# AdaLN block with gated linear attention: the six modulation vectors summed over their input rows on TensorE instead of on VectorE

## The reference

```python
mod = (silu(c) @ wmod).reshape(1, 6, 1, -1)          # wmod is 512 x 3072
sa, ca, ga, sb, cb, gb = (mod[:, n] for n in range(6))
ga = (2 * (ga >= 0) - 1) * maximum(abs(ga), 0.25)    # the same for gb
h = layernorm(x) * (1 + ca) + sa
x = x + ga * attention(h, Wq, Wk, Wv, Wo, Wg, Wog, Wd, bd, norm_w)
h = layernorm(x) * (1 + cb) + sb
x = x + gb * channel_mix(h, W_r, W_k, W_v, mu_r, mu_k)
```

## Time and profile before

| | us |
|---|---|
| median of three executions | 3675.05 |
| lowest and highest of them | 3674.24, 3677.36 |
| the profiled execution, its own time | 3674.58 |
| its span, first to last instruction | 3672.8 |
| PE busy | 3596.5 (98%) |
| DVE busy | 2145.5 (58%) |
| ACT busy | 1546.0 (42%) |
| POOL busy | 464.7 (13%) |
| mean granted clock of TensorE | 0.991 |

### The profile page before, as it was taken

How to read it: one execution, slowest core, us unless ns; L and a number is a source line. 1 busy time by engine, 2 the same in 40 slices (tenths; PEclk the granted TensorE clock), 3 DMA queues, 4 the chain that set the end, 5 groups by cost and what they waited for, 6 DMA issues and landing times. The chain is left out here.

```text
span 3672.8 us, 73725 instructions
## 1 busy us (share of the span) xinstructions
PE 3596.5 (98%) x25349; PEld 3339.3 (91%) x25349; DVE 2145.5 (58%) x5207; ACT 1546.0 (42%) x3904; POOL 464.7 (13%) x883
## 2 busy tenths in 40 slices
PE   7999999999999999999999997899999999999998
PEld 7999999999999999999999997688888888888887
DVE  4555555555555555555555556566566655666566
ACT  4445445445545445445445453333332323233332
POOL 0111111111111111111111111100000000000000
PEclk8999999999999999999999999899999999999999
DMA  4222322322322322322232223412221122212220
GB/s 156 76 60 65 81 60 58 87 62 56 87 63 55 86 64 54 81 71 54 75 77 54 75 71 87 162 69 71 77 91 69 69 80 85 75 69 74 75 91 23
DMA packets 206044, 274.89 MB, mean 75 GB/s; under 512 B 13968, under 2 KB 146080, under 8 KB 206000
## 3 DMA queue, kind: packets, MB, share of 16 engines
q1 hardware_dynamic: 206000, 274.31, 25.6%
HBM read 189.84 MB, written 84.41 MB: 75 GB/s over the span
## 5 line engine op out<-in xcount | busy, mean ns | idle before, releaser
L813 POOL TENSOR_TENSOR k_lo<-kg,k_hi 128x256 fp32r<-128x256 f32 x256 | 186.7, 729 | 1501.1 <-ACT q_hi L588 1501.1
L609 ACT ACTIVATE decay<-cum_rows,w_cur 128x128 f32<-128x128 f32 x1024 | 327.8, 391 | 20.6 <-POOL cum_rows L807 12.7
L55 PE MATMUL psJ<-h_hi,w_g_hi 128*128 128x256 f32 x1024 | 314.7, 307 | 8.3 <-DVE h_lo L675 4.6
L577 ACT COPY q<-psJ 128x256 f32<-128x256 f32 x256 | 95.5, 373 | 501.1 <-PE psJ L57 501.1
L55 PE MATMUL psJ<-h_hi,w_q_hi 128*128 128x256 f32 x1024 | 304.4, 297 | 0.0
L683 DVE SCALAR_TENSOR_TENSOR kg<-gate,psJ 128x256 f32<-128x256 f32 x256 | 107.8, 421 | 333.0 <-PE psJ L57 305.5
L56 PE MATMUL psJ<-h_lo,w_q_hi 128*128 128x256 f32 x1024 | 286.2, 279 | 0.0
L57 PE MATMUL psJ<-h_hi,w_k_lo 128*128 128x256 f32 x1024 | 286.1, 279 | 0.0
L56 PE MATMUL psJ<-h_lo,w_g_hi 128*128 128x256 f32 x1024 | 285.9, 279 | 0.0
L57 PE MATMUL psJ<-h_hi,w_q_lo 128*128 128x256 f32 x1024 | 285.8, 279 | 0.0
L55 PE MATMUL psJ<-h_hi,w_k_hi 128*128 128x256 f32 x1024 | 285.6, 279 | 0.0
(11 more groups left out here) (226 smaller groups left out, 10601.8 us busy)
## 6 DMA issues: line engine op xcount, KB each, us to landing
cum_rows<-cum_dram SPq DMA_DIRECT2D x256, 256.0 KB, 5.4
o_rows_dram<-o SPq DMA_DIRECT2D x256, 128.0 KB, 1.8
o_rows<-o_rows_dram SPq DMA_DIRECT2D x32, 1024.0 KB, 5.4
an_norm_x<-in_L_attn_x_dram SPq DMA_DIRECT2D x32, 512.0 KB, 3.9
h_dram<-h_hi SPq DMA_DIRECT2D x32, 512.0 KB, 2.7
h_dram<-h_lo SPq DMA_DIRECT2D x32, 512.0 KB, 3.8
h_hi<-h_dram SPq DMA_DIRECT2D x32, 512.0 KB, 3.7
h_lo<-h_dram SPq DMA_DIRECT2D x32, 512.0 KB, 4.6
```

The costliest lines, as they stand in the source:

```text
L55: nc.tensor.matmul(out, w_hi, x_hi, start=first, stop=False)
L577: nc.scalar.copy(q[:, b, :], psJ[USES.index(("q", b)) % 2][:, 0:T]).then_inc(s["by_act"], 1)
L609: last = nc.scalar.activation(decay[:, 2 * c + h, :], cum_rows[:, p % 4, 2 * c + h, :], ACT.Exp, bias=w_cur[:, 3, c, 2 * p + h:2 * p + h + ...
L813: nc.gpsimd.tensor_tensor(k_lo[:, :], kg[:, p, :], k_hi[:, :].bitcast(F32), ALU.subtract).then_inc(s["k_lo"], 1)
```

## The change

PE takes the staged modulation block itself. For each of the four columns b it accumulates four float32 matmuls, k = 0 to 3, with the 128 x 128 block b of row k as stationary operand and column k of silu(c), 128 x 1, as moving one. It waits for the load of the block in place of the sums, and in the first list also for silu(c). DVE's four operations for each vector, the tensor `sums` and the semaphore `sum` are gone. The lists of jobs, the buffers for staging, `finish_mod` and everything else stay.

```diff
@@ tensor, a modulation job
                     m = before(is_mod, n)
-                    pe.wait_ge(s["sum"], KD * (m + 1))
+                    pe.wait_ge(loaded[n % NS], 16 * (n // NS + 1))
+                    if first:
+                        pe.wait_ge(s["silu"], 1)
                     hold(pe, s["mod_out"], m - 1)
                     for b in range(KD):
-                        last = nc.tensor.matmul(mod_ps[m % 2][:, b:b + 1], sums[:, m % 2, b * P:(b + 1) * P],
-                                                t["ones"][:, 0:1], start=True, stop=True)
+                        for k in range(KD):
+                            last = nc.tensor.matmul(mod_ps[m % 2][:, b:b + 1], stage[n % NS][:, k, b * P:(b + 1) * P],
+                                                    t["silu_c"][:, k:k + 1], start=k == 0, stop=k == KD - 1)
                     last.then_inc(s["read"], 1)
@@ vector, a modulation job
                 if is_mod[n]:
-                    m = before(is_mod, n)
-                    dve.wait_ge(loaded[n % NS], 16 * (n // NS + 1))
-                    for k in range(KD):
-                        rows, weight = stage[n % NS][:, k, :], t["silu_c"][:, k:k + 1]
-                        if k == 0:
-                            if first:
-                                dve.wait_ge(s["silu"], 1)
-                            nc.vector.tensor_scalar(sums[:, m % 2, :], rows, weight, None, ALU.mult).then_inc(s["sum"], 1)
-                        else:
-                            dve.wait_ge(s["sum"], KD * m + k)
-                            nc.vector.scalar_tensor_tensor(out=sums[:, m % 2, :], in0=rows, scalar=weight, in1=sums[:, m % 2, :],
-                                                           op0=ALU.mult, op1=ALU.add).then_inc(s["sum"], 1)
                     if unfinished is not None:
                         finish_mod(unfinished)
                     unfinished = n
```

More of the change, by code:

```diff
@@ L84, in prepare @@
         sign = ctx.enter_context(nc.sbuf_tensor(f"{name}_sign", [P, 4, KD], F32))
-        sums = ctx.enter_context(nc.sbuf_tensor(f"{name}_sums", [P, 2, 512], F32))
         bank = [ctx.enter_context(nc.psum_tensor(f"{name}_ps{n}", [P, 512], F32)) for n in range(NB)]
         mod_ps = [ctx.enter_context(nc.psum_tensor(f"{name}_mod{n}", [P, 512], F32)) for n in range(2)]
-        s = signals(nc, ctx, name, "turned hi lo scaled read sum mod_out gate step "
+        s = signals(nc, ctx, name, "turned hi lo scaled read mod_out gate step "
                     "small filled masks exp one silu wd wd_hi mu")
```

## The result

The changed kernel takes 3680.04 us, the median of 22 executions (3676.11 to 3684.88); the kernel before in the same comparison 3675.19 (22 executions, 3672.5 to 3677.48). The ratio is 1.0014, with a 95% interval of 1.0008 to 1.0021. That is 4.9 us or 0.13% slower, clear of zero by the interval and under the 0.2% up to which the prediction calls a time the same. From the fastest to the slowest execution there are 8.8 us, where the kernel before has 5.0 here.

What follows compares the result with a forecast made beforehand. TensorE, busy 98% in the two untouched passes, was taken as the bound, so only the two prepare stages count: 3674.6 + 4.5 + 3.5 = 3682.6, forecast as 3682 us, own range 3679 to 3685, 8-in-10 range 3668 to 3686.5.

Steps and rivals of the forecast that it cites:

- signs of being wrong: Clock 1.00 during GA or CA, a pair not 0.216 or 0.108 us, or attention's start not moved 4 to 5 us.
- What is removed: VectorE's four operations per vector in both prepare stages: about 2.85 us each, 17 us for six.
- The price of a pair: Weight load plus one-column matmul on TensorE: 0.216 us at the low clock, 0.108 at the full one, no accumulation latency.
- the rival with the drain: Each accumulating pair waits for the last one's drain, 0.35 us a pair: 3700 us and more; chance 3%.
- Which clock: In both prepare stages, a long stream of one-column pairs was assumed not to raise TensorE's clock from 0.50.
- The rival with 25%: The stream raises the clock in the prepare stages: whole kernel -5.8 us, 3668.8 us; chance 25%.
- Second prepare, +3.5: GA and GB at the low clock, SB and part of CB at the full one: v2 starts 3.5 us later.
- five pairs are fast: In CB of the second prepare, five pairs at the full clock and 27 at the low one: 6.4 us.
- First prepare, +4.5: SA and CA both at the low clock, 13.8 us: k0 starts 4.15 us later, with slower banks +4.5 in all.
- The sum: Profiled time 3674.6 plus 4.5 for the first prepare and 3.5 for the second: 3682.6 us.

Runs made afterwards that it cites:

- e3: Changed kernel with silu(c) repeated over 64 moving columns in place of one: 3672.07 us, ratio 0.9992 to the kernel before.
- e4: Changed kernel with silu(c) repeated over 128 moving columns in place of one: 3667.94 us, ratio 0.9980 to the kernel before.
- e2: Kernel before with the change in the second prepare only (GA, GB, SB, CB): 3680.08 us, ratio 1.0011 to the kernel before.
- e1: Kernel before with the change in the first prepare only (SA, CA): 3676.55 us, ratio 1.0002 to the kernel before.
- e8: Changed kernel run once more with no edit, for a second profile: that execution took 3683.93 us.
- e6: Changed kernel with 128 columns plus 24 identity transposes on TensorE at the start of the second prepare: 3665.93 us, ratio 0.9974 to the kernel before.

## Why the prediction was right, and where not

The forecast was 3682 us with a range of its own from 3679 to 3685; 3680.04 was measured. The mechanism was the forecast's: the streams cost by the clock, and a one-column stream does not raise it. That the sum came out so near was partly luck: its term for the first prepare was too high and that for the second too low. Two of the prediction's own signs of being wrong are there: the granted clock was 1.00 in the first part of CA, and the first prepare, up to the start of the attention, changed by -0.9 and +2.0 us in the two profiles, not by 4 to 5. Step by step:

- **What is removed.** 17 us on VectorE were said, 17.3 left the page. That they save nothing by themselves beyond TensorE's wait held.
- **The price of a pair.** 0.216 us at 0.50 and 0.108 at 1.00: GA and GB took 13.67 us for 64 pairs (0.214 each), SA 3.5 us for 32 (0.109). The accumulation over four blocks added nothing, so the rival with the drain falls. The choice of the measured 0.216 us at the low clock was right. By the estimate from the page "TensorE: Matmul & The Clock Gate" of the Trainium skill, section "LDWEIGHTS (loading the stationary operand)", 107 ns for a load of 128 columns, GA and GB would have needed 6.8 us, about half of what they took.
- **Which clock.** Right that the stream doesn't raise it, at 13.7 us of GA and GB without a gap. The rival with 25%, that it does, is excluded by the same row. I had no row that decided it. Against that rival the prediction counts 2.7 us that TensorE filled at 0.50; the rows have 6.1 us, from the start of the second vector's pairs at 2317.6 in the trace of before through the transposes to the rise at 2323.7. What I had only assumed, that the moved columns make the difference, e3 and e4 now show: TensorE and the weight loads are busy 100% in these streams whatever the width, and the clock differs. In the sum of that rival, 1.0 us for the four banks of v2 should be 0.7 (four times 0.86 less 0.69); that changes nothing in the forecast.
- **Second prepare, +3.5.** The intermediate steps, counted from the landing of GA: og0 +6.3 (said +6.5), o0 +5.9 (+5.8), o1 +4.9 (+4.6), v2 +4.7 (+3.5), the end +4.3 (+3.5). The step that was somewhat off is "five pairs are fast" in CB and the start of SB: the clock fell right at the end of SB, so that SB and CB took 10.4 us instead of 9.9, and TensorE came to SB 0.6 us later than worked out. By the medians of e2 the stage costs 4.8, 1.3 more than said.
- **First prepare, +4.5.** This is the term of the sum that was mis-sized. It put both vectors at 0.50 from 20.9, because the clock had fallen at 19.8 in the trace of before. In the changed kernel it was at 1.00 until 24.3 in one profile, and until about 22 in the other: SA was mostly fast, CA mostly slow, 8.8 and 11.1 us instead of 13.8. The stage changed by -0.9 and +2.0 in the two profiles, and by +1.2 between the medians of e1, whose interval takes in zero. The place of a fall was read from one execution as if it belonged to the program, but it differs between executions: in the profile of e2, whose first prepare is that of the kernel before, the clock was at 1.00 from 17.9 to about 25 and not down at 19.8.
- **The sum.** 4.5 + 3.5 = 8 was said, 4.9 measured. By the medians of e1 and e2 the first term was 3.3 us too high and the second 1.3 too low, so that part of the first error is hidden; these two medians add up to 6.0, and the 1.1 us between them and the measured 4.9 is within their intervals. That the forecast lies within 2 us of the measured median owes something to leaving out the 0.5 us between the profiled execution and the median, too.

The cost that remains is shown: undoing the first stage leaves it (e2), and giving the same pairs more columns removes it and more (e4). In the kernel with 128 columns the change gains 3.0 us in the first prepare and 4.1 in the second by the profiles, a good quarter of the 26 us that TensorE had waited for VectorE in the earlier trace rows.

## What to carry to other kernels

In a stream of float32 matmuls, each with a 128 x 128 stationary block of its own, a pair with one moving column costs nearly as much at the full clock as one with 128 (0.109 against 0.113 us), and TensorE's clock fell to half in it; repeat the operand over 128 columns where the PSUM bank has room. Do not move small sums from VectorE to TensorE on the strength of TensorE's idle time alone: price the stream at both levels of the clock, and take as range what the place of a fall can make of it, since it differs from one execution to the next. Transposes in a wait for a DMA (24 of them here, 4 to 5 us) brought the clock back for the work behind them. With 128 columns it stayed; with one column, and 1.6 us of idle time between, it was lost at once.

## What the runs showed of the hardware

- TensorE busy 100% by matmuls and weight loads for 13.7 us did not bring the clock back from 0.50, with one moving column (changed, e2, e8) and with 64 (e3); with 128 it was back after 4.6 us (e4). The Trainium skill's page "TensorE: Matmul & The Clock Gate", section "The HAM clock gate", has busy-ness release the clock; here a busy TensorE was not enough.
- With 64 columns the clock stayed at 1.00 for all 7 us of SA with CA and of SB with CB; with one column it was lost in CA and after SB. The 64 columns are of one profile, in which the same pairs stayed at 0.50 in GA and GB.
- The clock rose during float32 transposes alone: it was at 0.50 when 24 of them began at 2282.43, and at 1.00 by the end (e6). The same page of the Trainium skill, in "PE-mode transpose", says that the full rate does not engage for them; the trace shows otherwise.
- The places of the clock's changes differ between executions, and the time with them: SA and CA took 8.8 and 11.1 us in two profiles of the changed kernel. The spread over the executions is 8.8 us with one column (22 executions), 6.3 with 128 (11) and 1.9 with 128 and the warm start (10). The kernel before has 4.6 to 8.8 in its four comparisons (15 to 33 executions), so only the 1.9 stands clearly apart.
